# Routed MLP with LayerNorm on one core: plain stores for each sequence in place of indexed scatters, and GpSimd's gamma before its power

## What is computed

```python
out_nr  = gelu(x @ w1_nr  + b1_nr)  @ w2_nr  + b2_nr          # 256 -> 256 -> 256
out_tsr = gelu(x @ w1_tsr + b1_tsr) @ w2_tsr + b2_tsr         # 256 -> 256 -> 256
h       = gelu(gelu(x @ w1_sr + b1_sr) @ w2_sr + b2_sr)       # 256 -> 512 -> 256
out_sr  = h @ w3_sr + b3_sr
out = where(c == 0, out_nr, where(c == 1, out_tsr, where(c == 2, out_sr, 0)))
y = x + out
result = (y - mean(y)) * rsqrt(var(y) + 1e-5) * gamma + beta   # over the 256 features
```

## Time and profile before

| | |
|---|---|
| Median of 3 runs | 112.78 us (111.09, 112.78, 112.89) |
| The profiled execution | 111.2 us |
| Its span, first to last instruction | 109.5 us |
| Busy PE, PEld, DVE, ACT, POOL in the span | 86.0, 74.9, 77.6, 64.3, 68.3 us |
| Mean granted TensorE clock | 0.949 |

### The profile page before, as it was taken

One profiled execution on the slowest core, in us unless ns is written; L12 is line 12 of the kernel. 1 busy time (PEld: TensorE's weight loads), 2 busy tenths in 40 slices (PEclk: granted clock), 3 DMA queues, 4 the chain that ended last, 5 costly groups with the idle time before them and its releaser, 6 DMA issues.

```text
span 109.5 us, 1829 instructions
## 1 busy us (share of the span) xinstructions
PE 86.0 (79%) x503; PEld 74.9 (68%) x503; DVE 77.6 (71%) x193; ACT 64.3 (59%) x104; POOL 68.3 (62%) x78
## 2 busy tenths in 40 slices
PE   0269969999999999999999999999999976600000
PEld 0157568868889888798998989989899866500000
DVE  5579084762555572839989899899998889699800
ACT  0575229995986045895977959779595870330000
POOL 6427910019777630000796988979879798999850
PEclk9999999999999999999999999999999999995555
DMA  0794788100498991000000404022040130103153
GB/s 2 264 311 142 234 258 298 34 0 3 94 343 205 419 407 73 0 6 0 0 6 22 175 3 174 6 87 105 6 192 6 73 130 6 54 0 154 40 216 144
DMA packets 5459, 12.84 MB, mean 117 GB/s; under 512 B 688, under 2 KB 2752, under 8 KB 5440
## 3 DMA queue, kind: packets, MB, share of 16 engines
q0 software_dynamic: 2880, 9.96, 25.5%
q1 hardware_dynamic: 2540, 2.63, 7.3%
q10 hardware_dynamic: 20, 0.01, 0.0%
HBM read 8.40 MB, written 4.72 MB: 120 GB/s over the span
## 4 chain that ended last, share of the span: by engine, by line
PE 67%; POOL 13%; DVE 4%; DMA 4%; issue 4%; POOLq 2%; ACT 1%; ACTq 1%
PE ps_a L732 8%; PE ps_a L734 8%; PE ps_a L733 7%; PE ps_x L713 7%; PE ps_f L786 6%; PE ps_f L788 6%; PE ps_f L787 6%; POOL xs L346 4%; POOL xs L341 4%; PE ps_f L814 4%; DMA bias_rows<-L_cond_b_sr_dram 4%; PE ps_f L777 3%; POOL rstd L331 3%; PE ps_b L807 2%; PE ps_b L808 2%
## 5 line engine op out<-in xcount | busy, mean ns | idle before, releaser
L331 POOL TENSOR_TENSOR rstd<-hvar,half 128x4 f32<-128x4 f32 x9 | 9.4, 1040 | 15.6 <-DVE hvar L598 15.5
L788 PE MATMUL ps_f<-wf_hi,f_hi 128*128 x64 | 17.9, 280 | 0.0
L786 PE MATMUL ps_f<-wf_hi,f_lo 128*128 x64 | 17.9, 280 | 0.0
L787 PE MATMUL ps_f<-wf_lo,f_hi 128*128 x64 | 17.9, 280 | 0.0
L732 PE MATMUL ps_a<-x_hi,w_lo 128*128 128x512 f32 x40 | 16.5, 413 | 1.1 <-DVE x_lo L643 1.1
L409 ACT ACTIVATE f_hi<-ps_a,bias_cols 128x512 fp32r<-128x512 f32 x16 | 11.0, 688 | 9.6 <-PE ps_a L808 4.7
L734 PE MATMUL ps_a<-x_hi,w_hi 128*128 128x512 f32 x40 | 15.7, 393 | 0.0
L733 PE MATMUL ps_a<-x_lo,w_hi 128*128 128x512 f32 x40 | 15.6, 390 | 0.0
L299 POOL DMA_INDIRECT xs<-x_dram,load_idx x11 | 11.1, 1012 | 6.5 <-DVE load_idx L538 3.6
L413 ACT ACTIVATE xs<-xs,shift,rstd 128x256 f32<-128x256 f32 x23 | 12.1, 593 | 4.3 <-POOL shift L335 4.3
L346 POOL TENSOR_TENSOR xs<-xs,beta_b 128x768 f32<-128x768 f32 (+1 forms) x8 | 14.1, 1762 | 0.5
(11 more groups left out here) (124 smaller groups left out, 191.3 us busy)
## 6 DMA issues: line engine op xcount, KB each, us to landing
w_raw<-L_cond_w_sr_dram SPq DMA_DIRECT2D x2, 512.0 KB, 4.6
wf_raw<-L_cond_w_sr_dram SPq DMA_DIRECT2D x1, 256.0 KB, 5.3
w_raw<-L_cond_w_tsr_dram SPq DMA_DIRECT2D x1, 256.0 KB, 6.5
w_raw<-L_cond_w_nr_dram SPq DMA_DIRECT2D x1, 256.0 KB, 6.8
wf_raw<-L_cond_w_tsr_dram SPq DMA_DIRECT2D x1, 256.0 KB, 6.9
wf_raw<-L_cond_w_nr_dram SPq DMA_DIRECT2D x1, 256.0 KB, 7.1
xs<-x_dram,load_idx POOLq DMA_INDIRECT x11, 6.5
out_dram<-xs,store_idx POOLq DMA_INDIRECT x9, 3.4
```

The source lines that it names most:

```text
L331: nc.gpsimd.tensor_tensor(rstd[:, g, :], hvar[:, g, :], half[:, :], ALU.pow).then_inc(rstd_step, 1)
L786: nc.tensor.matmul(dst, fl[:, kt, toks], w_hi, start=False, stop=False)
L787: nc.tensor.matmul(dst, fh[:, kt, toks], w_lo, start=False, stop=False)
L788: mm = nc.tensor.matmul(dst, fh[:, kt, toks], w_hi, start=False, stop=last)
```

## The change

1. The indexed scatters and `store_idx` go. SP stores each group with eight plain DMAs, one for each sequence (16 partitions of 4 KB to 64 KB of `out`), whose destination comes from a register and which is left out where the place is empty. For the last group SP issues the first four and ACT the other four.
2. The destination table `place_tab` (sequence and taken flag of each of 88 places) is made at the start: three more constants by GpSimd (`CONSTS` = 13), two more operations and a copy by DVE, two more matmuls by PE, which stand ahead of the ten warm-up matmuls. For each group SP loads eight flags and eight sequence numbers from the table into registers (ACT four and four, once).
3. GpSimd applies gamma of group g-1 ahead of root(g); beta stays behind it. In the last step it takes three tiles of group 7 in place of two, and DVE one in place of two; ACT's variant for that group goes.
4. The control flow is written differently: steps below `MIN_GROUPS` run without a branch on their slot; from slot 8 on each step begins with a branch between `finish` of the group before and the normal step, with `finish` first in the code. The last layer of the group before, and the normalisation beside it, now stand in each branch of the long and the short route.

The core of the diff ("..." marks what is left out):

```diff
+    PLACES = SLOTS * PER
-        store_idx = sb("store_idx", [P, SLOTS], I32)
+        place_id = sb("place_id", [B, PLACES])
+        seq_ones = sb("seq_ones", [B, 2])
+        place = sb("place", [B, 1])
+        at_place = sb("at_place", [B, PLACES])
+        place_tab = sb("place_tab", [1, 2, PLACES], I32)
-        CONSTS = 10
+        CONSTS = 13
...
+        def load_places(eng, regs, row, s, first, n, hi):
+            eng.load(regs[0:n], place_tab[0:1, row, s * PER + first:s * PER + first + n])
+            return [eng.snap(r, min_val=0, max_val=hi) for r in regs[0:n]]
+        def out_of(seq):
+            return out[bass.ds(seq, 1), :, :].rearrange("a (q t) h -> (a q) t h", t=TT)
+        def rows_of(s, j):
+            return xs[s][j * ROWS:(j + 1) * ROWS, :, :]
+        def each_step(eng, cls, step, finish):
+            for s in range(SLOTS + 1):
+                if s < MIN_GROUPS:
+                    step(s)
+                elif s < SLOTS:
+                    with eng.If(cls[s] > NR):
+                        if s == MIN_GROUPS:
+                            finish(s - 1)
+                        else:
+                            with eng.If(cls[s - 1] < EMPTY):
+                                finish(s - 1)
+                            with eng.Else():
+                                pass
+                    with eng.Else():
+                        step(s)
...
         @block.sync
+            sp.wait_ge(place_tab_done, 1)
             sp.wait_ge(tab_done, 1)
             cls = load_classes(sp, "sp_cls")
+            def store(g, n):
+                taken = load_places(sp, taken_regs, 1, g, 0, n, 1)
+                seqs = load_places(sp, seq_regs, 0, g, 0, n, B - 1)
+                if n == PER:
+                    sp.wait_ge(o_pool, g + 1)
+                sp.wait_ge(o_dve, 2 * (g + 1))
+                for j in range(n):
+                    sp.dma_start(out_of(seqs[j]), rows_of(g, j), cond=(taken[j] > 0)).then_inc(stored[g], 16)
+            def sp_step(s):
+                if s > 0:
+                    store(s - 1, PER)
+            each_step(sp, cls, sp_step, lambda g: store(g, PER // 2))
...
         @block.gpsimd
+            nc.gpsimd.iota(place_id[:, :], [[1, PLACES]], base=0, channel_multiplier=0, ...
+            nc.gpsimd.iota(seq_ones[:, 0:1], [[0, 1]], base=0, channel_multiplier=1, ...
+            nc.gpsimd.memset(seq_ones[:, 1:2], 1.0).then_inc(consts, 1)
-            def scatter(g, last):
...
+            def pool_group(g):
+                if g > 0:
+                    times_gamma(g - 1, POOL_TT)
                 root(g)
                 shifted(g)
                 if g > 0:
-                    times_gamma(g - 1, POOL_TT)
                     plus_beta(g - 1, POOL_TT)
-                    scatter(g - 1, False)
+            def pool_finish(g):
+                times_gamma(g - 1, POOL_TT)
                 root(g)
+                plus_beta(g - 1, POOL_TT)
...
         @block.scalar
+            def act_finish(g):
+                normed(g - 1)
+                n = PER // 2
+                taken = load_places(act, taken_regs, 1, g, n, n, 1)
+                seqs = load_places(act, seq_regs, 0, g, n, n, B - 1)
+                act.wait_ge(o_dve, 2 * (g + 1))
+                for j in range(n):
+                    act.dma_start(out_of(seqs[j]), rows_of(g, n + j), cond=(taken[j] > 0)).then_inc(stored[g], 16)
...
         @block.vector
             nc.vector.tensor_copy(cls_tab[:, :], cls_f[:, :]).then_inc(tab_done, 1)
+            chain(nc.vector.scalar_tensor_tensor(out=place[:, :], in0=base[:, :], scalar=float(PER), in1=rank[:, :],
+                                                 op0=ALU.mult, op1=ALU.add))
+            nc.vector.tensor_scalar(at_place[:, :], place_id[:, :], place[:, 0:1], None, ALU.is_equal
+                                    ).then_inc(at_place_done, 1)
+            dve.wait_ge(places_ps, 1)
+            nc.vector.tensor_copy(place_tab[:, :, :], places_pt).then_inc(place_tab_done, 1)
...
         @block.tensor
+            pe.wait_ge(at_place_done, 1)
+            nc.tensor.matmul(places_pt[:, 0, :], seq_ones[:, 0:1], at_place[:, :], start=True, stop=True)
+            nc.tensor.matmul(places_pt[:, 1, :], seq_ones[:, 1:2], at_place[:, :], start=True, stop=True
+                             ).then_inc(places_ps, 1)
             for i in range(WARM):
                 nc.tensor.matmul(ps_f[:, 0, :], ones2[:, :], warm_x[:, :], start=True, stop=True)
             transpose_x(0)
...
+            def pe_step(s):
                 if s > 0:
+                    pe.wait_ge(x_lo_done, upto_x(s))
+                    if_next(pe, cls, s, transpose_x)
+                with pe.If(cls[s] < TSR):
+                    long_first(s)
+                    if s > 0:
+                        last_layer(s - 1, ps_f)
+                    long_second(s)
+                with pe.Else():
+                    with pe.If(cls[s] < NR):
+                        short_first(TSR, s)
                     with pe.Else():
+                        short_first(NR, s)
+                    if s > 0:
+                        last_layer(s - 1, ps_f)
+            each_step(pe, cls, pe_step, lambda g: last_layer(g, ps_x))
```

More of the change, by code:

```diff
@@ L211, in load_classes, with x_of, if_next @@
             return [eng.snap(r, min_val=0, max_val=EMPTY) for r in regs]
[L213 to L220, removed]
+        def load_places(eng, regs, row, s, first, n, hi):
+            eng.load(regs[0:n], place_tab[0:1, row, s * PER + first:s * PER + first + n])
+            return [eng.snap(r, min_val=0, max_val=hi) for r in regs[0:n]]
+        def x_of(seq):
+            return x[bass.ds(seq, 1), :, :].rearrange("a (q t) h -> (a q) t h", t=TT)
+        def out_of(seq):
[15 more added lines that the diff above has]
+                                pass
                     with eng.Else():
-                        last(g)
+                        step(s)
                 else:
[L224 to L230, removed]
-                with eng.Else():
[L232 to L237, removed]
+                    with eng.If(cls[s - 1] < EMPTY):
+                        finish(s - 1)
+                    with eng.Else():
+                        pass
+        def if_next(eng, cls, s, part):
+            if s + 1 < MIN_GROUPS:
+                part(s + 1)
+            elif s + 1 < SLOTS:
+                with eng.If(cls[s + 1] < EMPTY):
+                    part(s + 1)
+                with eng.Else():
+                    pass
         @block.sync
@@ L362, in middle, with pool_step_of @@
                 if g > 0:
-                    times_gamma(g - 1, POOL_TT)
                     plus_beta(g - 1, POOL_TT)
-                    scatter(g - 1, False)
-            def final(g):
-                times_gamma(g - 1, 2)
-                root(g)
[L370 to L378, removed]
+            def pool_step_of(s):
+                if s > 0:
+                    pool_group(s - 1)
+            def pool_finish(g):
+                times_gamma(g - 1, POOL_TT)
+                root(g)
+                plus_beta(g - 1, POOL_TT)
+            each_step(pool, cls, pool_step_of, pool_finish)
         @block.scalar
@@ new lines, in norm_part, with dve_step_of @@
+            def norm_part(s):
+                if s >= 1:
+                    middle(s - 1)
+                if s == 2:
+                    dve.wait_ge(gamma_done, 1)
+                if s >= 2:
+                    gamma_beta_one(s - 2)
+            def dve_step_of(s):
+                f, f_l = f_hi[s % 2], f_lo[s % 2]
+                if s > 0:
+                    if_next(dve, cls, s, x_low)
+                with dve.If(cls[s] < TSR):
+                    banks = (ps_a[0], ps_a[1], ps_b, ps_a[0])
+                    for m in range(HT):
+                        low(banks[m][:, 0, :], h_hi[:, m, :], h_lo[:, m, :], HID * s + m + 1, 1)
+                        if s == 0 and m == 0:
+                            x_low(1)
+                    if s == 0:
+                        w_low(2)
+                        w_low(3)
+                    norm_part(s)
+                    for m, bank in ((0, ps_a[1]), (1, ps_b)):
+                        low(bank[:, 0, :], f[:, m, :], f_l[:, m, :], HID * s + HT + m + 1, 1)
+                with dve.Else():
+                    if s == 0:
+                        w_low(2)
+                        w_low(3)
+                    for m in range(2):
+                        low(ps_a[m][:, 0, :], f[:, m, :], f_l[:, m, :], HID * s + SHORT[m], SHORT_STEP[m])
+                        if s == 0 and m == 0:
+                            x_low(1)
+                    norm_part(s)
@@ L698, in _ @@
+            each_step(dve, cls, dve_step_of, final)
         @block.tensor
```

205 lines of the change are left out of this document (55 added, 150 removed).

## The result

| | before | after |
|---|---|---|
| Median of 4 runs of each | 112.03 us (111.09 to 112.89) | 120.13 us (119.67 to 121.01) |
| Profiled execution | 111.2 us | 119.67 us |
| Its span | 109.5 us | 117.9 us |
| Mean granted TensorE clock | 0.949 | 0.917 |

What follows compares the result with a forecast made beforehand. PE was taken to bound the kernel between start and tail, SP's queue the new tail. Start +2.0 and tail +2.9, stall gain included, made +4.9 on the median 112.78: 117.7 us, range 112.3 to 122.

Steps and rivals of the forecast that it cites:

- case A: The forecast itself: SP issues serially in the tail, d between 0.36 and 0.55, 115.1 to 120 us; chance 0.48.
- E: Rival: new long jumps hold PE, at step 8 or up to 1.2 us in several steps; 118 to 124; chance 0.04.
- d: SP's time for one store with flag and address from registers: taken as 0.46 us, bounds 0.28 to 0.83.
- start: Before the first layer: constants and two place matmuls ahead of the warm-ups; +2.0 us, between 1.2 and 3.0.
- loads: SP's register loads, two per group ahead of the wait: 1.2 us for eight registers, 0.95 for four.
- the middle: Middle steps: no change, as PE has no gaps and GpSimd's saving and the branches hide behind it; 0 us.
- The tail: From DVE's last work to the end: SP's stores and loads in a row; +4.2, or +2.9 with the stall's gain.
- Case C: Rival: from d = 0.56 on SP bounds the whole kernel; 122.1 at d 0.6, about 135 at 0.8; chance 0.16.
- The stall at `ps_x`: PE between groups 7 and 8: its wait goes, since `finish` stands directly behind step 8; 1.5 us gone.
- The moments of group 8: DVE's stretch from its first `ps_x` addition of group 8 to the start of `hvar`: no growth, 0 us.

Runs made afterwards that it cites:

- e1: Kernel after, with ACT issuing all eight stores of the last group and SP none: 116.70 us, ratio 1.048 to the kernel before.
- e5: Kernel after, with stores to fixed rows, without flags, address registers or register loads; output order differs: 115.31 us, ratio 1.038 to before.
- f1: Kernel before, with one unused tile of 128 bytes per partition ahead of the x tiles, moving operands from 192 to 64 modulo 256: 112.16 us, ratio 1.009.
- f3: Kernel after, with ACT issuing the last group's eight stores, place matmuls behind the first transposes, and 128 bytes of pad: 114.97 us, ratio 1.036 to before.
- e4: Kernel after, with GpSimd's indexed scatters back and no place table; new control flow, gamma ahead of root and third tile stay: 113.68 us, ratio 1.023 to before.
- f2: Kernel before, with only GpSimd's gamma of group g-1 moved ahead of root(g) in the middle steps: 112.32 us, ratio 1.013.

## Why the prediction was right, and where its sizes were off

**What would happen, and where.** The forecast was case A, with SP serial in the tail. It came true in direction and mechanism: 120.1, just above A's own range (115.1 to 120) and inside the range given. e1 shows the mechanism by moving the work off SP, e5 by making it cheaper. The number alone wouldn't tell A from E (118 to 124), and A's own condition, d between 0.36 and 0.55, did not hold.

**Luck in the number.** The growth was forecast as 4.9 us and the span grew by 8.4. The forecast of 117.7 came closer to 120.1 only because I added the 4.9 to 112.78, the median of three runs; added to the 111.2 of the profiled execution, it is 116.1. And the terms missed in both directions: start and loads were too dear, the store and the middle too cheap.

**The tail, +6.5 in place of +4.2.** The failed term is d. I took 0.46 for a store with register address and flag, the short issue of the earlier trace rows plus 0.22, for which I had no row. The store takes 0.635. The 0.22 was near (0.17 by e5); the base was wrong: I used the duration of one short issue, 0.24, as the distance of two, and a store with a constant address takes 0.46 (e5). My bounds, 0.28 to 0.83, held it. Against the forecast's end of 114.4 the account is: store(6) starts 0.9 late (its data 0.6), 19 distances of 0.635 in place of 0.46 make +3.3, one issue of 1.14 and the gap behind it +1.2, the loads 1.8 and 1.1 in place of 2.4 and 1.9 make -1.4 (0.52 and 0.30 for a load, where proportion from 11 registers gave 1.2 and 0.95), and what follows the last issue took 2.5 in place of 3.1, -0.6. Together +3.4, and the span ended 3.5 after 114.4; the data's own delay of 1.2 taken off, that is the 2.3 between 6.5 and 4.2.

**Case C, SP as the bound of the whole kernel,** came within 0.3 us of happening. With d at 0.635 and the cheaper loads a full group costs SP 6.66 (first store of group 2 at 72.78, of group 3 at 79.43), under the step of 7.0. But SP had little slack: one issue of 0.99 made a group cost 7.32, it began the stores of groups 2 to 5 between 0.7 and 1.0 us behind GpSimd's beta (0.3 where it waits for it), and caught up behind group 5, which has two sequences. My threshold of 0.56 was too low because the loads were overpriced, and C's sum took every group as full.

**The start, +1.27 in place of +2.0.** The warm-ups came 2.5 later in the chain (forecast 2.2): `at_place` was done at 9.09 (forecast 8.9), and the two matmuls took 0.75 (0.7). The clock gave back 1.2 of it, 0.6 in the warm-ups and 0.6 in the transposes. I had set its bound at 0.8 because I counted the warm-ups alone and took the transposes behind them as fixed. That it gave back 1.2 is this execution's: in e1, with the same start, the first layer began at 16.64, +2.1, and next to nothing came back.

**The middle, 0, was wrong** in two ways that add to +1.4. The matmuls' distance went from 0.2297 to 0.2335 with the address of their operand (f1: 1.0 us), a side effect of the new tiles that no row of before could show. And the new control flow has a branch of 3.3 us in the first short step, of which 0.4 is seen (7.46 for the step, 7.02 in f1). I had taken that branch at 0 because PE's matmuls lie queued ahead of it, and had given it rival E with 0.04; all ten versions with the new flow have it, and it costs up to 1.6 us (f3). The rule of the Trainium skill that I had cited (Runtime: NRT & Kernel Launch, Instruction fetch mechanics: a taken branch out of the fetched window waits for its page) fits the first jump, and deserved more weight; why the later jumps over the same block take only 0.33 to 0.48, it doesn't tell. I expected the stall at step 8, where the longest jump is; there no branch took over 0.48. One of 5.1 us came behind PE's last matmuls, where it held nothing.

**The stall at `ps_x`, 1.5 us gone: right.** PE has no wait there after. Together with the loss in the middle this makes +0.21 for the body, so the stall gave about 1.2.

**The moments of group 8, 0, were wrong:** +1.19. `diff` was held 1.68 in place of 0.48 us, by GpSimd's gamma. DVE's gain from the stall was given back whole. In the kernel after this cost the end nothing, since SP began the stores of group 7 2.9 us after their data and was 7.9 us late at group 8; where the end follows the data, as in e4 and f2, it counts. I treated an engine with spare time as free to move; f2 shows that moving it costs 1.2 us in the old kernel too. In the kernel after only the last step is hit, since without the scatters gamma is over before the moments in the steps before it.

**What stays open.** Which part of the change of control flow makes the branch long was not tried, only that all versions with the new flow have it. That the hold on DVE is a port and not something else rests on the end times that agree and on the rule of the Trainium skill given below. SP's long single issues (0.99 to 1.14 us, three in the kernel after; 1.69 the longest in e5) have no cause here, nor has the moment at which the clock's level rises, nor the 0.7 us behind the last scatter of the new flow.

## What to carry to other kernels

Count the instructions on each queue behind the last data, loads and address steps included, and price a store by its distance to the next, not by the shortest issue that the trace shows: one scatter of 1.05 us on GpSimd was replaced by eight stores of 0.635 and two loads. Before an engine's spare time is used, look at what else runs beside the new place, since a large GpSimd operation can hold a DVE operation of 0.17 us for as long as it lasts. And after adding a small tile or a branch, compare the distance of two matmuls and the longest branch with those of before, because here both changed though the step's own work did not.

## What the runs showed of the hardware that was not expected

- **DVE held by GpSimd.** A DVE `tensor_tensor` with both inputs in SBUF that starts beside GpSimd's 128x768 `tensor_tensor` ends with it: 1.68 us in the kernel after (101.04, gamma 101.02), 0.66 in f2 (73.46 and 73.43), 0.48 before (98.37, beta 98.35), where 0.166 is the median. In e4 one of 2.59 us starts beside the scatter and ends with gamma (101.46 and 101.43). The next operations on 128x4 elements take their usual 0.15. The Trainium skill (SBUF — State Buffer, Who interferes with whom) states that a DVE instruction with two SBUF inputs contends with a GpSimd instruction that reads SBUF, and that the port pair they share is an exclusive lock; the end times of all four pairs agree.
- **Matmul distance and address.** 512 columns: 0.2297 us with the moving operand at 192 modulo 256 bytes, 0.2335 at 64, 1.6% of every such matmul.
- **A plain store from SP's queue:** 0.46 us apart with a constant address, 0.635 with address and flag in registers, 0.39 left out by its flag, landing 1.9 us. Eight registers from SBUF 0.52, four 0.30, eleven 1.36.
- **Branches of PE's queue:** 0.33 median, but 3.3 to 4.3 us at the first jump over the long route in the new flow, and 4.5 to 5.3 at a jump behind its last layer. The old flow has 2.1 to 2.8 at the jump ahead of its last layer.
